# The residual of the chunk inverse: its f16 copy in a tile of its own, the masked operand written from it, and the instruction order planned anew

## The reference, cut to what matters

```
S = S * exp(gt)
delta = (vt - kt @ S) * bt
S = S + outer(kt, delta)
o = (qt * scale) @ S
```

## Time and profile before

| | |
|---|---|
| median of 3 runs | 4367.94 us (4365.03 to 4368.02) |
| the profiled execution, its own time | 4369.75 us |
| its span, first to last instruction | 4367.4 us |
| PE busy | 4283.0 us, 98% |
| DVE, ACT, POOL busy | 2910.0, 2473.9, 1528.8 us |
| mean granted TensorE clock | 0.996 of full speed |

### The profile page before, as it was taken

One profiled execution on the slowest core, in us unless ns is written; L12 is line 12 of the kernel. 1 busy time (PEld: TensorE's weight loads), 2 busy tenths in 40 slices (PEclk: granted clock), 3 DMA queues, 4 the chain that ended last, 5 costly groups with the idle time before them and its releaser, 6 DMA issues.

```text
span 4367.4 us, 85716 instructions
## 1 busy us (share of the span) xinstructions
PE 4283.0 (98%) x31800; PEld 3226.7 (74%) x31800; DVE 2910.0 (67%) x6454; ACT 2473.9 (57%) x6254; POOL 1528.8 (35%) x1686
## 2 busy tenths in 40 slices
PE   7999999999999999999999999999999999999998
PEld 5778778777677777777777777777777777777775
DVE  4555555554676777777777676677777777766675
ACT  1222222222576666666666666666676667666664
POOL 2222222222233333333333333334443344434434
PEclk8999999999999999999999999999999999999999
DMA  4100100002100000000000011011111111111111
GB/s 133 34 22 29 31 19 28 31 21 79 46 18 26 23 24 21 23 21 21 22 22 22 22 62 40 26 57 35 45 38 35 35 35 38 38 35 35 45 30 47
DMA packets 115518, 154.69 MB, mean 35 GB/s; under 512 B 32416, under 2 KB 59040, under 8 KB 115104
## 3 DMA queue, kind: packets, MB, share of 16 engines
q1 hardware_dynamic: 79008, 93.97, 6.5%
q10 hardware_dynamic: 36096, 55.24, 4.1%
HBM read 113.76 MB, written 35.42 MB: 34 GB/s over the span
## 4 chain that ended last, share of the span: by engine, by line
PE 49%; issue 10%; POOL 6%; DVE 6%; ACT 3%; POOLq 0%; DVEq 0%; ACTq 0%
PE bank L1066 11%; PE bank L1062 10%; PE bank L1634 8%; PE bank L1356 7%; PE bank L1480 2%; PE bank L1568 2%; PE bank L1542 2%; PE bank L1528 2%; PE bank L1503 2%; POOL ktok L1146 1%; PE bank L1195 1%; DVE errh L1435 1%; POOL rnk L1140 1%; POOL rnq L1189 1%; DVE pt L1303 1%
## 5 line engine op out<-in xcount | busy, mean ns | idle before, releaser
L1062 PE MATMUL bank<-xtile,wt 128*128 128x259 f32 x4096 | 1121.5, 395 | 4.3 <-PEq L652 2.5
L1062 PEld LDWEIGHTS bank<-xtile,wt 128*128 128x128 f32 x4096 | 711.1, 191 | 123.5 <-issue 59.0
L1413 ACT ACTIVATE xyinv<-bank 128x512 f16<-128x512 f32 x768 | 448.1, 592 | 220.5 <-PE bank L1356 217.5
L1634 PE MATMUL bank<-wot,xnt 128*128 128x512 f32 x1024 | 540.4, 613 | 0.8 <-ACT xnt L1627 0.8
L1066 PE MATMUL bank<-wt,xtile 128*128 128x512 f32 x1024 | 536.9, 618 | 0.0
L1389 DVE TENSOR_TENSOR wlev<-bank,mask 128x256 f16<-128x256 f32 x768 | 315.8, 417 | 201.6 <-PE bank L1356 199.9
L1092 DVE SCALAR_TENSOR_TENSOR vraw<-bank,taps,vraw 128x256 f32<-128x256 f32 x768 | 363.7, 477 | 69.0 <-ACT vraw L1085 56.0
L1333 POOL TENSOR_TENSOR kend<-ktok,gts 128x256 f32<-128x256 f32 x256 | 152.9, 618 | 722.6 <-issue 722.5
L440 PE MATMUL bank<-hb,wt 128*128 128x128 f32 x2816 | 375.2, 277 | 11.8 <-POOL hb L410 6.4
L440 PEld LDWEIGHTS bank<-hb,wt 128*128 128x128 f32 x2816 | 349.1, 193 | 34.3 <-issue 21.5
L1356 PEld LDWEIGHTS bank<-xyinv,lth 128*128 128x128 f16 x3584 | 220.4, 97 | 177.0 <-issue 99.1
(11 more groups left out here) (191 smaller groups left out, 9208.6 us busy)
## 6 DMA issues: line engine op xcount, KB each, us to landing
grows<-row_scratch ACTq DMA_DIRECT2D x126, 256.0 KB, 3.2
xtile<-xt_scratch ACTq DMA_DIRECT2D x30, 518.0 KB, 3.7
xn<-x SPq DMA_DIRECT2D x32, 256.0 KB, 4.0
xt_scratch<-xt SPq DMA_DIRECT2D x16, 512.0 KB, 4.2
g_scratch<-sel SPq DMA_DIRECT2D x32, 256.0 KB, 2.0
part_scratch<-prow SPq DMA_DIRECT2D x32, 256.0 KB, 2.0
prow<-part_scratch SPq DMA_DIRECT2D x32, 256.0 KB, 2.6
sel<-g_scratch SPq DMA_DIRECT2D x32, 256.0 KB, 2.9
```

The source lines that it names most:

```text
L1062: j = pe.matmul(b_p[:, 0:WIN], wt[:, k, c:c + P], xtile[:, par, k, :], **st)
L1413: act.activation(dst, b_inv[p][:].rearrange("p (a h b s) -> p a h b s", a=2, h=HEADS, s=z), ACT.Copy).then_inc(s[f"xy_sb{p}"], 1)
L1634: i = pe.matmul(b_o[:], xnt[:, h], wot[:, h], start=(h == 0), stop=(h == GV - 1))
```

## The change

A new tile `errd` holds ACT's f16 copy. DVE masks it out of place into `errh` first, and computes `errl` from it second; before, `errl` came first and the mask waited for it and worked in place. ACT's copy no longer waits for `pe_third` of unit n - 1, and DVE's mask does instead. The planner's dependences follow, and its duration of DVE's pair goes from 1.12 to 1.14, from which all four engines' orders are computed anew. The f16 identity leaves the table of masks, so that the masks behind it move, and the six copies that fill `wlev` at the start read the f32 identity.

```diff
-M_LT, M_LE, M_ID, M_NEG, M_L0T, M_OFF, M_EVEN = range(7)
+M_LT, M_LE, M_OFF, M_NEG, M_L0T, M_EVEN = range(6)
...
-    c[:, C_ID] = m[:, M_ID] = np.eye(P)
+    c[:, C_ID] = np.eye(P)
+    m[:, M_OFF] = 1.0 - np.eye(P)
     m[:, M_NEG] = -SCALED * np.eye(P)
-    m[:, M_OFF] = 1.0 - np.eye(P)
...
-        errh, errl = (sb(n, [P, HEADS, P], F16) for n in ("errh", "errl"))
+        errd, errh, errl = (sb(n, [P, HEADS, P], F16) for n in ("errd", "errh", "errl"))
...
-                dve.tensor_copy(wlev[:, lv], mask[:, M_ID, :].unsqueeze(1).broadcast_to([P, HEADS, P])).then_inc(c_set, 1)
+                dve.tensor_copy(wlev[:, lv], ident.unsqueeze(1).broadcast_to([P, HEADS, P])).then_inc(c_set, 1)
...
             if n:
-                act.wait_ge(s[f"c3_ps{1 - p}"], (n - 1) // 2 + 1)
                 act.wait_ge(s["el_sb"], 2 * n)
-            act.activation(errh[:], quad(b_inv[p]), ACT.Copy).then_inc(s["eh_sb"], 1)
+            act.activation(errd[:], quad(b_inv[p]), ACT.Copy).then_inc(s["eh_sb"], 1)
...
             dve.wait_ge(s["eh_sb"], n + 1)
-            dve.tensor_tensor(errl[:], quad(b_inv[n % 2]), errh[:], ALU.subtract).then_inc(s["el_sb"], 1)
-            dve.wait_ge(s["el_sb"], 2 * n + 1)
-            dve.tensor_tensor(errh[:], errh[:], mask[:, M_OFF, :].unsqueeze(1).broadcast_to([P, HEADS, P]), ALU.mult).then_inc(s["el_sb"], 1)
+            if n:
+                dve.wait_ge(s[f"c3_ps{1 - n % 2}"], (n - 1) // 2 + 1)
+            dve.tensor_tensor(errh[:], errd[:], mask[:, M_OFF, :].unsqueeze(1).broadcast_to([P, HEADS, P]), ALU.mult).then_inc(s["el_sb"], 1)
+            dve.tensor_tensor(errl[:], quad(b_inv[n % 2]), errd[:], ALU.subtract).then_inc(s["el_sb"], 1)
...
-                ("act", "error"): [("pe", "error", n), ("pe", "third", n - 1), ("dve", "error", n - 1)],
-                ("dve", "error"): [("act", "error", n)],
+                ("act", "error"): [("pe", "error", n), ("dve", "error", n - 1)],
+                ("dve", "error"): [("act", "error", n), ("pe", "third", n - 1)],
...
-            ... ("dve", "error"): 1.12, ...
+            ... ("dve", "error"): 1.14, ...
```

More of the change, by code:

```diff
@@ L1820, in attention @@
             ("dve", "conv"): 0.50, ("dve", "keys"): 0.70, ("dve", "gate"): 0.50, ("dve", "scores"): 0.70, ("dve", "decay"): 1.22, ("dve", "lower"): 0.69, ("dve", "attend"): 0.69,
-            ("dve", "start"): 0.42, ("dve", "level"): 0.42, ("dve", "error"): 1.12, ("dve", "second"): 0.69, ("dve", "third"): 0.69,
+            ("dve", "start"): 0.42, ("dve", "level"): 0.42, ("dve", "error"): 1.14, ("dve", "second"): 0.69, ("dve", "third"): 0.69,
             ("dve", "recall"): 1.13, ("dve", "learn"): 1.13, ("dve", "answer"): 0.87, ("dve", "out"): 0.70,
```

## The result

The changed kernel takes 4330.96 us (median of 4 runs, 4329.69 to 4338.62), the kernel before 4366.48 us in the runs beside it (4363.91 to 4368.02). The ratio is 0.9923, with a 95% interval of 0.9906 to 0.9940: 0.8% faster. The forecast was 0.5% faster, 4347 us, in a range of 4333 to 4393.

What follows compares the result with a forecast made beforehand. PE, busy 98% of the span, was taken as the bound. Profiled 4369.75 - 23 (two waits) + 2 (order) = 4348.75; runs' median 1.8 lower, so 4347 us, 0.5% less; range 4333 to 4393, likeliest case 4338 to 4353.

Steps and rivals of the forecast that it cites:

- Mask first: DVE's error pair: mask starts ahead of POOL's `pool_low`, pair ends 0.72 us earlier at 2567.93, and PE's two waits go.
- A: First of two recurring PE waits for masked `errh`, behind four L1062 records; priced at 0.49 us a period.
- What the two waits cost PE: PE's two waits for masked `errh`: together 0.78 us a period, times 29.5 periods, 23 us.
- B: Second recurring PE wait for masked `errh`, behind two L1062 records; priced at 0.29 us a period.
- D: Not in the prediction: place 1.5 us behind the first `errh` wait, PE's keys' transposes (L1111) behind DVE's convolution.
- The order: New planned order on all four engines, called the unknown; taken as a small loss of 2 us.
- C: PE wait for `wlev` behind two 512-column records, 0.54 us; if it went too, 16 us more gain.
- Constants: Six startup copies reading f32: at most 2.8 us more, under DVE's 3.16 us of idleness, so zero.
- POOL's delay: `pool_low` late by 0.21 us if the mask stops it; nothing waits, 6 us kept for the range.
- Rival 1: New order adds three or more PE waits per tile, costing more than it saves: 4393 us; chance 0.25.
- rival 2: Mask, moved 0.7 us forward, still meets POOL instructions, so no change: 4366 us; chance 0.13.
- Rival 3: Half given back: a B-sized wait stays, or PE reaches the `wlev` wait earlier: 4356 us; chance 0.17.

Runs made afterwards that it cites:

- first experiment: Changed kernel's code with the planner given the old dependences and 1.12, so all engines keep the order of before: 4334.54 us, ratio 0.9921 to the kernel before.
- third kernel: Own tile, out-of-place mask, moved wait and order of before, but subtraction first and mask second: 4368.64 us, ratio 1.0000 to the kernel before.

## Why the prediction was right in kind and too small

**Mask first.** Right, as the first and third kernels show, and for the reason given: the mask ends before or just after `pool_low` asks for the port. At A it was forecast to start when the subtraction had, and to be done as `pool_low` comes; that is what the timeline has.

**The step that failed** is "What the two waits cost PE", and with it the count of who waits. It gave 0.49 + 0.29 = 0.78 us a tile. Two errors are in it:

- *A was 0.58 and not 0.49.* I deducted 0.10 us for the change from f32 to f16. The side by side shows that the group behind the four records starts in 0.88 us with nothing to wait for, and 4 x 0.2175 is 0.87: there is no such cost at this place, where the four stand behind f32 work (L1619). The six records that I took it from stand behind f16 work. So do the two at B, which take 0.52 us for 2 x 0.2175 = 0.435 in the experiment, and B was right to 0.01 (0.29 forecast, 0.30 measured). At these places the extra 0.1 us thus goes with the change into f32, and not with that out of it. For A that is 0.09 x 29.5 = 3 us.
- *D was missing.* I priced what waits for the pair on PE and didn't ask what is queued behind it on DVE. The convolution is, and PE's transposes with it: 0.14 x 29.5 = 4 us.

**The order** was put at a loss of 2 us and is nothing: at the same clock the changed kernel and the first experiment differ by about 1 us. That is luck in part: the prediction counted on an order close to the old one, and the new one isn't. The sum with the measured sizes is 4368 - 30 = 4338, which is what the changed kernel takes in its one run at clock 0.995 (4338.62 us). The median is 8 us lower because its three other runs had 0.997, and no term of the prediction was for that. Why more of its runs have 0.997 than of the kernel before stays open: three of four, with five of eight of the program with the same code and the old order, against three of nineteen.

**The range** reached down only by C's price. An error of 30% in the likeliest case's own term (23 us for 30), and runs that differ by 8 us with the clock, were not in it.

**Out of place** at no cost: right (third kernel, 1.0000). **The moved wait** at no cost: right, DVE's new wait for the third product doesn't show. **Constants** at no cost: the six copies from f32 have records of 419 ns where the f16 form had 288, and DVE was still idle behind them, for 0.68 us. **POOL's delay**, kept for the range: no loss found. Forecast was 0.21 us at B, measured is 0.06, and over all 128 L1322 has a mean of 1.17 us for 1.16.

**Rival 1** (a costlier order) and **rival 2** (still meeting POOL) didn't happen. Rival 2's mechanism is real, though: it is what the experiment with the mask done twice shows, and the third kernel. **Rival 3** (PE reaches C earlier and waits longer there) didn't happen either: the loads' waits for `wlev` are 50.4 us and 50.4 us in the first experiment, which has the same order, and 54.5 in the changed kernel.

## What to carry to other kernels

Where one instruction has two durations, lay its slow cases beside the engine that shares a resource with it, and look which of the two can be made to start first: here a swap of two lines, or one wait on another engine, was worth 31 to 35 us. Price a late result twice, once for who waits for it and once for what stands behind it on its own engine. And a planner that is given durations without the delays by other engines leaves waits that look like bad luck; a longer duration for one delayed operation, its measured mean or somewhat more, was worth another 19 to 24 us here.

## What was not expected of the hardware

The meeting goes by the same sum in both directions: the second operation loses what the first has left, less 0.14 us. Of the 65 masks that start behind `pool_low` in the kernel before, each is late by that sum to 0.01 us (at A 0.85 left and 0.70 lost, in the mask done twice up to 0.98 lost: 1.40 us for 0.42). `pool_low` behind a mask takes 1.22 us for 1.16 where 0.20 us of the mask are left, 1.34 where 0.32 are left. So the short operation should go first: it can cost the long one 0.28 us at most by this sum, and loses up to 0.98 behind it. The Trainium skill (SBUF — State Buffer, "SBUF: two separate sides") says that whoever starts first has the shared port pair for the whole instruction, and that the other stands still. The trace agrees with the order of starts in both directions, but for the 0.14 us by which the two records overlap beyond that.

Not every POOL instruction stops the mask. In the changed kernel nine masks start while L1608 runs, a power of 128x4 elements that takes 1.0 us. They take 424 to 426 ns, one of them with 0.85 us of L1608 left. Here the measurement and the Trainium skill's "for the whole instruction" (same section) differ, and a busy POOL alone is no sign of a meeting.

An f16 mask right before a subtraction from PSUM overlaps it in the records: at A the mask starts at 2553.21 for 0.41 us and the subtraction already at 2553.54, so the pair takes 1.01 us. In the old sequence, with the wait between the two, it takes 0.68 + 0.03 + 0.42 = 1.13 us where POOL is idle.
